# Who adds up the band scores of batch 0, when the scattered rows go out, and which queue carries the maximum rows

## What is computed

```
xn = layernorm(x)
q, k, v = (xn @ Wq + bq) / 4, xn @ Wk + bk, xn @ Wv + bv      # 16 heads of 16 channels
w = q k^T; w[t, s] += q[t] . emb_rel_k[s - t + 4]  for |s - t| <= 4
p = softmax(w); a = p v, plus p[t, s] * emb_rel_v[s - t + 4] on the same band
moe = sum over the top 2 of 8 experts: weight * (silu(xn w1) * (xn w3)) w2
out = x + a Wo + bo + moe
```

## Time and profile before

| | us |
|---|---|
| median of 3 runs (lowest, highest) | 2137.64 (2135.26, 2139.28) |
| the profiled execution | 2146.0 |
| its span, first to last instruction | 2144.1 |
| stage `attention` in it | 196 to 1249 |
| stages of the experts and the end | 1249 to 2144 |

### The profile page before, as it was taken

How to read it: one execution, slowest core, us unless ns; L and a number is a source line. 1 busy time by engine, 2 the same in 40 slices (tenths; PEclk the granted TensorE clock), 3 DMA queues, 4 the chain that set the end, 5 groups by cost and what they waited for, 6 DMA issues and landing times. The chain is left out here.

```text
span 2144.1 us, 36132 instructions
## 1 busy us (share of the span) xinstructions
PE 1800.1 (84%) x11121; PEld 1026.0 (48%) x11121; DVE 1506.6 (70%) x2627; ACT 1103.0 (51%) x2115; POOL 773.5 (36%) x529
## 2 busy tenths in 40 slices
PE   6992328888888889899988859999999999999992
PEld 4761002222222223233322227777777777778882
DVE  3765677666666667777766239888888888898552
ACT  3541005565666566566688854444445454445550
POOL 1002899755444544400000013534444354443111
PEclk9985559999999999999999979999999999999996
DMA  5998997555543344233455156776767677675655
GB/s 181 344 347 269 250 295 208 156 134 138 143 128 104 104 137 101 77 79 69 110 165 176 40 202 224 228 228 214 247 210 237 211 231 232 212 251 168 201 166 166
DMA packets 227567, 395.56 MB, mean 184 GB/s; under 512 B 15440, under 2 KB 161760, under 8 KB 219296
## 3 DMA queue, kind: packets, MB, share of 16 engines
q1 hardware_dynamic: 193088, 279.97, 43.5%
q0 software_dynamic: 25824, 93.73, 14.3%
q10 hardware_dynamic: 8576, 20.97, 2.7%
HBM read 306.37 MB, written 87.99 MB: 184 GB/s over the span
## 5 line engine op out<-in xcount | busy, mean ns | idle before, releaser
L736 DVE CUSTOM_DVE_ANT_0 t_seen<-t_s,hide 128x1024 bf16<-128x1024 f32 x512 | 603.4, 1221 | 285.8 <-PE t_s L623 282.4
L804 ACT ACTIVATE t_pr<-t_s 128x512 f32<-128x512 f32 x1024 | 560.6, 604 | 329.2 <-PE t_s L636 231.5
L632 PE MATMUL t_s<-t_q,t_k 98*128 98x512 bf16 x1024 | 366.2, 392 | 95.6 <-DMA t_q<-t_mt 63.6
L623 PE MATMUL t_s<-t_k,t_q 96*128 96x512 bf16 x1024 | 331.5, 407 | 97.5 <-DVE t_mx L736 71.7
L1349 ACT ACTIVATE e_sg<-e_pa,e_down 128x256 f32<-128x256 f32 x312 | 148.0, 474 | 424.5 <-PE e_pa L1224 412.4
L1420 DVE SCALAR_TENSOR_TENSOR e_wl<-e_ws,e_up,e_wh 128x512 f16<-128x512 f32 x312 | 320.0, 1038 | 13.6 <-ACT e_wh L1310 0.5
L1233 PE MATMUL e_py<-e_w2s,e_hT 128*128 128x256 f32 x1248 | 324.3, 383 | 1.0 <-DVE e_hT L1442 1.0
L632 PEld LDWEIGHTS t_s<-t_q,t_k 98*128 98x128 bf16 x1024 | 97.8, 98 | 437.4 <-ACT t_pr L804 260.5
L1224 PE MATMUL e_pa<-e_xh,e_wh 128*128 128x256 f16 x1248 | 239.4, 274 | 49.0 <-DVE e_xl L1412 41.9
L647 PE MATMUL t_po<-t_pr,t_vx 128*32 128x512 f32 x2048 | 279.7, 619 | 0.7 <-ACT t_pr L804 0.7
L1224 PE MATMUL e_pa<-e_xh,e_wl 128*128 128x256 f16 x1248 | 238.7, 273 | 0.0
(11 more groups left out here) (202 smaller groups left out, 1857.5 us busy)
## 6 DMA issues: line engine op xcount, KB each, us to landing
e_ws<-in_L_ffn_w_dram SPq DMA_DIRECT2D x78, 1024.0 KB, 4.9
e_w2s<-in_L_ffn_w_dram SPq DMA_DIRECT2D x39, 1024.0 KB
e_vs<-v_rows POOLq DMA_DIRECT2D x32, 1152.0 KB, 5.8
t_kw<-k_rows POOLq DMA_DIRECT2D x22, 1152.0 KB
t_q<-q_stack SPq DMA_DIRECT2D x32, 768.0 KB, 6.1
t_k<-k_stack SPq DMA_DIRECT2D x32, 768.0 KB, 9.0
t_kw<-in_L_ffn_w_dram ACTq DMA_DIRECT2D x16, 1024.0 KB, 4.9
t_kw<-k_rows SPq DMA_DIRECT2D x10, 1152.0 KB, 7.3
```

The costliest lines, as they stand in the source:

```text
L623: last = nc.tensor.matmul(s1[:, buf, half * CH:(half + 1) * CH], q1[0:ROWS, u, h, i * P:(i + 1) * P], k1[0:ROWS, u, h, half * CH:(half + 1 ...
L632: last = nc.tensor.matmul(s2[:, bank, :], k2[0:ROWS + MROWS, u, h, i * P:(i + 1) * P], q2[0:ROWS + MROWS, u, h, half * CH:(half + 1) * CH] ...
L736: nc.vector.tensor_tensor_reduce(out=seen[:, buf, :], in0=s1[:, buf, :], in1=c["hide"][:, (TB - 1 - i) * P:(TB - 1 - i) * P + L], scale=1. ...
L804: nc.scalar.activation(pr[:, k % BP, n % HG], s2[:, turn(u, n)], ACT.Exp).then_inc(exp_ok, 1)
```

## The change

- `PIECES` is 3. For the 8 windows of batch 0, GpSimd only multiplies; VectorE sums the channels with three `tensor_reduce` instructions (`channel_sums`, each over 3 of the 9 shifts, 768 values into 48), put between the tiles of group 0. SyncE's next window load waits for these.
- For the 24 later windows GpSimd multiplies and folds as before, but starts window t only after VectorE's chain of group (t - 8) // 2. For all 32 windows the addition to `band` moves from VectorE to GpSimd (`add_to_band`). VectorE keeps the maximum over the shifts (`band_maximum`).
- All 64 scatters (`send`) come after the last window.
- The 13 zero fills move behind the loads of steps 0 and 1 of SyncE's queue, the fill of the expert sums behind those of step 9.
- ScalarE, having copied the maximum rows, waits for its own copy and issues the two DMAs itself. SyncE no longer does.

```diff
-    PIECES, FOLDS = 2, 4
+    PIECES, FOLDS = 3, 4
...
-                sp.wait_ge(zero_ok, 2)
                 for t in range(2, TB + 2):
-                    sp.wait_ge(sum_ok, t - 1)
+                    sp.wait_ge(part_ok, PIECES * (t - 1))
                     load_window(sp, t, t % 2, win_early)
-                    for z in range((t - 2) * N_ZERO // TB, (t - 1) * N_ZERO // TB):
-                        sp.dma_start(zeros[z], zero[:].broadcast_to([P, 6, XE])).then_inc(zero_out, 16)
-                sums = dr["moe"].rearrange("(n p) e -> p n e", p=P)
-                sp.dma_start(sums, zero[:, :, 0:E].broadcast_to([P, NT + 1, E])).then_inc(sums_out, 16)
-                maximum(0, 0)
                 load2(1, 0, 1, 1)
...
-                    maximum(g + 1, 1 - u)
...
                 step(0, 0, 2, 0)
+                sp.wait_ge(zero_ok, 2)
+                for z in range(N_ZERO // 2):
+                    sp.dma_start(zeros[z], zero[:].broadcast_to([P, 6, XE])).then_inc(zero_out, 16)
                 step(1, 0, 3, 1)
+                for z in range(N_ZERO // 2, N_ZERO):
+                    sp.dma_start(zeros[z], zero[:].broadcast_to([P, 6, XE])).then_inc(zero_out, 16)
                 with sp.Fori(0, NB - 2) as r:
...
+                sp.dma_start(sums, zero[:, :, 0:E].broadcast_to([P, NT + 1, E])).then_inc(sums_out, 16)
                 step(10, 3, 0, 0)
...
+                def add_to_band(t, u):
+                    scores = band[:, t, :, :].rearrange("p m h -> p (m h)")
+                    nc.gpsimd.tensor_tensor(scores, scores, dot[:, u, :], ALU.add).then_inc(band_ok, 1)
+                    pool.wait_ge(band_ok, t + 1)
...
+                products(0, 0, 0)
+                for t in range(TB):
+                    if t < TB - 1:
+                        products(t + 1, (t + 1) % 2, (t + 1) // 2)
+                    pool.wait_ge(part_ok, PIECES * (t + 1))
+                    add_to_band(t, t % 2)
+                for t in range(TB, NT):
+                    pool.wait_ge(mparts_ok, (t - TB) // 2 + 1)
+                    products(t, t % 2, t // 2)
+                    fold(t, t % 2)
+                    if t < NT - 2:
+                        load_window(pool, t + 2, t % 2, win_in)
+                    add_to_band(t, t % 2)
                 for t in range(NT):
+                    send(t)
...
+                def channel_sums(t, u, piece):
+                    M = NM // PIECES
+                    if piece == 0:
+                        dve.wait_ge(mul_ok, t + 1)
+                        after(dve, band_ok, t - 1)
+                    nc.vector.tensor_reduce(
+                        dot[:, u, piece * M * H:(piece + 1) * M * H],
+                        kw[:, u, piece * M * E:(piece + 1) * M * E].rearrange("p (q d) -> p q d", d=D),
+                        AX.X, ALU.add).then_inc(part_ok, 1)
...
+                        if g0 and n % HG > 0:
+                            channel_sums(n // HG, n // HG % 2, n % HG - 1)
+                        elif g0 and n // HG > 1:
+                            band_maximum(n // HG - 2)
+                        elif not g0 and n in (X1 // 2, X1 - 4) and TB + 2 * (g - 1) < NT:
+                            band_maximum(TB + 2 * (g - 1) + (0 if n == X1 // 2 else 1))
...
-                def keep_maximum(g):
+                def keep_maximum(g, u):
                     act.wait_ge(mt_ps_ok, g + 1)
                     after(act, m_in, 16 * MROWS * g)
                     nc.scalar.copy(mt[:], s1[0:2 * HG * TB, 0, 0:P // 2].bitcast(BF16)).then_inc(mt_ok, 1)
+                    act.wait_ge(mt_ok, g + 1)
+                    for j in range(MROWS):
+                        act.dma_start(q2[ROWS + j:ROWS + j + 1, u].rearrange("o h (i t) -> o (h i) t", t=P),
+                                      mt[j * HG * TB:(j + 1) * HG * TB, :]).then_inc(m_in, 16)
```

More of the change, by code:

```diff
@@ L501, in load2 @@
                     sp.dma_start(vx[:, u], vd[b, gg]).then_inc(vin[u], 16)
[L503 to L508, removed]
                 zeros = dr["xs"].rearrange("(z r p) e -> z p r e", p=P, r=6)
@@ L543, in _ @@
                         step(4 * r + 2 + v, r + 1, v, v % 2)
+                sums = dr["moe"].rearrange("(n p) e -> p n e", p=P)
+                sp.dma_start(sums, zero[:, :, 0:E].broadcast_to([P, NT + 1, E])).then_inc(sums_out, 16)
                 step(10, 3, 0, 0)
@@ L559, in _, with products @@
                 xn_v = dr["xn"].rearrange("(c i p) e -> c p i e", p=P, i=CT)
-                def window_products(t, u, k, more=True):
+                def products(t, u, k):
                     if t < TB + 2:
@@ L708, in _, with band_maximum @@
                 neg_v = neg[:].rearrange("p (b i) (g h) -> p b g h i", i=TB, h=HG)
-                def window(t, u, piece):
+                def channel_sums(t, u, piece):
+                    M = NM // PIECES
                     if piece == 0:
[L714 to L720, removed]
+                        dve.wait_ge(mul_ok, t + 1)
[4 more added lines that the diff above has]
+                        AX.X, ALU.add).then_inc(part_ok, 1)
+                def band_maximum(t):
+                    dve.wait_ge(band_ok, t + 1)
+                    nc.vector.tensor_reduce(bmax[:, t, :], band[:, t, :, :].rearrange("p m h -> p h m"),
+                                            AX.X, ALU.max).then_inc(bmax_ok, 1)
                 def maxima(b, v):
@@ L727, in maxima @@
                     g, u = NG // NB * b + v, v % 2
-                    g0, more = isinstance(b, int) and g == 0, not isinstance(b, int) or b < NB - 1
+                    g0 = g == 0
                     for n in range(X1):
                         h, i, buf = n // TB, n % TB, n % B1
[L731 to L734, removed]
+                        if g0 and n % HG > 0:
[4 more added lines that the diff above has]
+                            band_maximum(TB + 2 * (g - 1) + (0 if n == X1 // 2 else 1))
                         dve.wait_ge(s1_ok, g * X1 + n + 1)
@@ L738, in maxima @@
                             scale=1.0, scalar=LOW, op0=ALU.add, op1=ALU.max, accum_out=mx[:, h, i:i + 1]).then_inc(mx_ok, 1)
+                    if g0:
+                        band_maximum(TB - 2)
+                        band_maximum(TB - 1)
                     dve.wait_ge(mx_ok, (g + 1) * X1)
@@ L745, in maxima @@
                     nc.vector.tensor_tensor(neg_v[:, b, v], mparts[:, 0], mparts[:, 1], ALU.add).then_inc(mparts_ok, 1)
[L747 to L752, removed]
                 nc.vector.memset(mparts[:], 0.0).then_inc(zeros_ok, 1)
@@ L822, in _ @@
                 final = NG // NB - 1
-                keep_maximum(0)
+                keep_maximum(0, 0)
                 exps(0, 0)
```

14 lines of the change are left out of this document (6 added, 8 removed).

## The result

The changed kernel takes 2064.28 us (median of 4 runs, 2059.9 to 2064.52) against 2138.46 us (2135.26 to 2141.22) of the kernel before in the same comparison. The ratio is 0.9649 [0.963, 0.9668]: 74.2 us less. That is faster, as forecast, inside the range, and 21.8 us above the forecast value. In the profiled execution (2064.3 us, span 2062.5) the attention ends at 1167.8 us instead of 1249.1.

A forecast was written before the change was run, and what follows sets the result against it. TensorE was taken as the bound, slowed by late maximum rows and the low clock after waits, with group 0 a second bound; 16.4 + 11.6 + 6 + 57.6 + 4.3 + 1.2 - 2 = 95.1 us gave 2042.5 us, range 2030 to 2066.

The forecast's parts named there:

- Pace of group 0: Group 0's maxima, with channel sums on VectorE, end at 292.5 instead of 308.9 us: 16.4 us gained.
- rival C: VectorE's channel sums are held beside GpSimd's products or slow; group 0's 16.4 us are lost: 2059 us, chance 0.08.
- I keep that: In group 0, window 2 arrives only at 236.15 us, behind load1 and load2, as before; its product ends at 241.2.
- 5.3 us in place of 16.9: Group 0's end of maxima to pass 2, with ScalarE issuing the rows and fills moved: 11.6 us gained.
- Borders: Window loads and scatters leave the group borders, rows come sooner: eight groups gain 57.6 us, group 9 4.3, group 0 6.
- W: Experiments' theory: window loads and scatters at the border made the maximum rows late, not the queue that carried them.
- Rival B: Rows come late all the same over the shared DMA engines; only group 0's gains remain: 2109 us, chance 0.06.
- of 1.1 us some 0.5 is left: ScalarE's row issues at step 56, partly hidden by idle gaps between exponentials, leave groups of 52.6 us.
- Rival A: ScalarE's issue is paid in full, 0.7 to 1.5 us in 13 groups: 2051 to 2062 us, chance 0.17.
- costed at nothing: The 64 late scatters, 85 us of GpSimd, are over before 1010 with 145 us of cover left: no cost.
- Fills: Zero fills moved behind load2 in groups 1 and 2, 14 to 28 us each with 40 us of cover: no cost.
- Rival D: Slower than before: ScalarE's issue blocks on a full queue, about 11 us in each of 16 groups: 2218 us, chance 0.03.

The follow-up runs named there:

- e7: Changed kernel with the 13 zero fills and the fill of the expert sums back in group 0: 2062.15 us, ratio 0.9655.
- e8: Changed kernel with batch 0's channel sums back on GpSimd (product, folds, addition to the band): 2075.72 us, ratio 0.9718.
- e1: Changed kernel with SyncE issuing the maximum rows again, behind load1, for group 0 ahead of load2: 2094.0 us, ratio 0.9763.
- e5: e1 with the 64 scatters spread between the windows instead of in one burst: 2046.97 us, ratio 0.9578.
- e6: Kernel before with one wait more: GpSimd starts windows from 10 on only after an earlier VectorE chain: 2096.27 us, ratio 0.9806.
- e2: Kernel before with one part of the change alone, ScalarE issuing the maximum rows: 2142.27 us, ratio 0.9981.
- e11: e4 with ScalarE issuing the rows and SyncE holding load1 (and group 1's load2) until they are there: 2053.79 us, ratio 0.9582.
- e4: e3 with SyncE issuing the maximum rows ahead of load1, for group 0 ahead of load2: 2042.56 us, ratio 0.9518.
- e9: Changed kernel without its 64 scatters, that part of the computation left out: 2057.37 us, ratio 0.9601.
- e3: Changed kernel with the 64 scatters spread behind windows 14 to 31 instead of all after the last: 2059.12 us, ratio 0.9596.
- e10: e4 with the scatters spread from window 12 on instead of 14: 2057.12 us, ratio 0.9599.
- e12: e4 with all scatters in one burst after the last window: 2086.41 us, ratio 0.9735.

## Why the prediction was right in sign and range, and too low by 22 us

Of the 20.9 us between 95.1 forecast and 74.2 measured, 7.5 are no part of the mechanism: the profile of before was that much above its own median (2146.0 against 2138.46), which the text had said of its sum, and the changed kernel's profile was at its median. Between the two profiled executions the gain is 81.7 us, 13.4 less than the sum.

**Pace of group 0: right mechanism, size too small.** The chain ends 89.4 us after the stage's start instead of 113.2: 23.8 us gained, 16.4 forecast. The reductions were sized rightly (0.95 us, 0.97 forecast) and not held, though the addition of two inputs was (5.12 us beside a product, 0.31 alone); rival C falls. The Trainium skill (GPSIMD Engine Reference, Key points) names two SBUF inputs or a 2-port mode as what contends, and the trace agrees: the addition with two inputs was held, the reduction with one was not. Two terms were too long. A window's next load was taken at 6.6 us, and SyncE's window loads landed in 5.7 us in the median; from the product of window 2 to that of window 6 that makes 31.9 us instead of 35.0. The text had this end in its bounds. The other was "I keep that", the start of the product of window 2, 40.4 us after the stage's start; it came after 37.2:

```profile
234.65 5.03 POOL L561 TENSOR_TENSOR t_kw<-t_kw,t_qw 128x2304 f32<-128x2304 f32 x1 [12.73 <-DMA t_kw<-k_rows]
```

That is 3.2 us more, which no bound had. Its cause was not tested, but the moved fills are not it, since e7 has 37.3. e8 prices the part by itself at 15 us.

**First rows: the step that failed is "5.3 us in place of 16.9".** They took 9.7 us from the chain's end to pass 2, because window 9 and load2 were already issued and load1 was on its way; with SyncE issuing the rows between window 9 and load2 the same stretch takes 3.4 (e1) and 4.7 us (e5). The text had named that case (a start at 303) and not taken it; it came in part, since the chain ended earlier. With the larger gain of the pace, the two errors cancel: pass 2 began at 296.5, and 297.8 was forecast.

**Borders: right.** The 63.6 us fell to 16.3. The forecast of under 8 us in all failed by group 0's 9.4; without that one and the two waits beside the scatters, 1.9 us are left. W is shown from two sides: pacing alone brings 41.5 us with the old queue (e6), the new queue alone brings 4 us with the old windows (e2). Since e6 moves window loads and scatters together, which of them it was is argued from group 10 of the kernel before (under e6) and not shown. Rival B, that the rows come late all the same, named the right law and the wrong price: the queue indeed made no difference, 4.0 us landing from either with load1 in flight and 1.9 us with nothing ahead. By the Trainium skill (DMA: Bandwidth & Descriptors, Issuing engines are not separate DMA queues) DMAs of different issuers interleave on the same 16 engines. The trace agrees, with 1.8/4.0/4.7 us from SyncE (e1) beside 1.8/4.0/8.2 from ScalarE.

**Groups of 52.6 us: the step that failed is "of 1.1 us some 0.5 is left".** From pass 2 of group 0 to that of group 12 the changed kernel takes 642.2 us, 53.3 a group without the scatter's wait of 2.42. So 0.7 us in each of 12 groups is missing, 8 us. The pair of issues measured 1.2 us, not 1.1, and e11 against e4 shows that 0.8 of it is paid in each group, where the forecast had 0.55: 3 of the 8 us. Waits for the rows at three borders, taken at nothing, are 1.9 more. Some 3 us stay unexplained. The idle 0.32 us between fours of exponentials did not hide it. My reading, argued and not shown: those gaps are the turns in which TensorE makes the next scores, and a stop of ScalarE only delays that turn. Rival A was right in kind, at 0.8 us a group near the lower end of its 0.7 to 1.5.

**Last batch and the scatters: the step that failed is "costed at nothing".** From the transpose of group 12 (930.13) to the stage's end the kernel loses 9.1 us, and 2 were forecast. The scatters did run where they were put (898.8 to 1001.6, over before 1010) and hold up no later stage; but the cover named was GpSimd's time, and the price fell on the others: waits of 2.42 and 2.58 us for the maximum rows and a group of 57.1 us. e9 and e3 price it at 10 and 11 us by their ratios; in the profiles the same stretch, from the transpose of group 12 to the stage's end, is 5.5 us shorter in e9 and 8.3 in e3.

**Fills: right.** They cost SyncE's queue 22.9 and 26.1 us in groups 1 and 2, and no group grew longer. That they help in group 0 was not claimed apart from the rows' path, and e7 shows that they do not.

**Rival D** (slower, ScalarE's issue blocks) falls: no issue took over 0.622 us. It decided from 6 us a group.

In sum, over the forecast by steps: pace +7.4, first rows -4.4, groups 0 to 11 -8.1, late groups -7.1; 1.7 us more were lost ahead of the attention, which began at 197.4 instead of 195.8, and 0.4 came back behind it.

## What to carry to other kernels

When a small transfer is urgent, look at what is in flight when it is issued: put the large loads behind it by the program's order, and do not expect another engine's queue to carry it past them. Do not put the issue on the engine that takes turns with the bound one; 1.2 us of issues there cost 0.8 us each time. And when work is moved "under cover", price what it does to the transfers of the others, not only its own engine's time.

## What the runs showed of the hardware that was not expected

- A burst of 64 indirect scatters, one each 1.27 us, makes other engines stand still for up to 6.5 us with "remote" or "issue" as the only reason, in two groups of 65.8 and 84.2 us (e1), when SyncE also issues the maximum rows. With ScalarE issuing them no wait is marked "remote" (the changed kernel, e7, e8) and the burst costs 5 to 10 us. Why the issuer matters here is not settled, and no run tells it apart.
- In all four kernels with the rows first (e4, e10, e11, e12) ScalarE stands still for over 7 us in group 8, with scatters beside it (e4) and without (e12), and whoever issues the rows (e11). It would be worth another 8 us (60.05 against 52.0). Its cause stays open.
- How strongly the landing of a small transfer depends on what was issued just before it: 1.9 us with nothing ahead (e4, e11), 4.0 with load1, from either queue, and up to 8.2 from ScalarE's with a window and load2 as well.
